# Convolution and two attentions on one core: the transformed image stored with its pixel column outside, and a new order of calls

## What is computed

```python
# block 0, image by image
perceived = conv3x3_depthwise(x, w_perc) + b_perc          # 3 filters a channel: 384 maps
hid = gelu(w_up1 @ perceived + b_up1)                      # 256
x_new = x + w_up2 @ hid + b_up2                            # 128
q, k, v = w_qkv @ x_new + b_qkv
w = softmax(q . k over the 3x3 neighbours / sqrt(128))     # zero-padded borders
h = x_new + sum(w * v)
# block 1
xn = group_norm(h, 8 groups) * gamma + beta
q, k, v = xn @ Wq + bq, xn @ Wk + bk, xn @ Wv + bv
out = softmax(q k^T / sqrt(128)) v @ Wp + bp               # 1024 x 1024 an image
y = xn + out
```

## Time and profile before

| | |
|---|---|
| three runs | 1112.1, 1113.34, 1116.12 us, median 1113.34 |
| the profiled execution | 1112.2 us, span 1110.4 us |
| mean granted clock of PE | 0.996 of 2.4 GHz |
| busy share PE, DVE, ACT, POOL | 96%, 81%, 70%, 39% |
| matmuls | 7488, of which 1728 are the convolution's, 1536 the values' |
| one turn of the loop | 65.97 us |

### The profile page before, as it was taken

One profiled execution on the slowest core, in us unless ns is written; L12 is line 12 of the kernel. 1 busy time (PEld: TensorE's weight loads), 2 busy tenths in 40 slices (PEclk: granted clock), 3 DMA queues, 4 the chain that ended last, 5 costly groups with the idle time before them and its releaser, 6 DMA issues.

```text
span 1110.4 us, 22840 instructions
## 1 busy us (share of the span) xinstructions
PE 1067.4 (96%) x7488; PEld 979.2 (88%) x7488; DVE 901.5 (81%) x1907; ACT 779.4 (70%) x1515; POOL 438.5 (39%) x399
## 2 busy tenths in 40 slices
PE   6979999999999999999999999999999999999897
PEld 5968989899898999989899898989989899998786
DVE  7868788888888878888887878888888887887875
ACT  4476767767676777767777676776767677776664
POOL 4656152542715345261532615254271534523021
PEclk9999999999999999999999999999999999999999
DMA  6001010100201010010100101010010100000000
GB/s 106 1 1 20 1 30 10 29 10 0 38 0 28 9 28 10 0 38 0 28 9 5 32 0 28 9 28 9 0 38 0 28 9 9 11 1 20 1 11 29
DMA packets 85746, 18.60 MB, mean 17 GB/s; under 512 B 67536, under 2 KB 85712, under 8 KB 85712
## 3 DMA queue, kind: packets, MB, share of 16 engines
q1 hardware_dynamic: 84992, 17.77, 8.3%
q10 hardware_dynamic: 720, 0.39, 0.2%
HBM read 9.76 MB, written 8.39 MB: 16 GB/s over the span
## 4 chain that ended last, share of the span: by engine, by line
issue 44%; PE 28%; POOL 20%; DVE 4%; ACT 3%; POOLq 1%; DMA 0%; DVEq 0%; ACTq 0%
PE work L457 7%; PE work L459 6%; PE work L458 6%; POOL g_lo L1295 6%; POOL t_lo L1295 3%; PE ps_t L614 3%; POOL v_hl L1295 2%; POOL h_lo L1295 2%; POOL xn_lo L1295 2%; PE ps_s L457 2%; PE ps_s L459 2%; PE ps_s L458 1%; POOL r_tok L1357 1%; POOL r_tok L1354 1%; POOL t_f L1312 1%
## 5 line engine op out<-in xcount | busy, mean ns | idle before, releaser
L1295 POOL TENSOR_TENSOR g_lo<-u,g_hi 128x512 fp32r<-128x512 f32 x60 | 77.8, 1303 | 375.1 <-ACT g_hi L890 375.1
L1749 DVE TENSOR_REDUCE nm<-ps_s 128x1 f32<-128x1024 f32 x124 | 151.4, 1221 | 32.5 <-PE ps_s L459 32.2
L457 PE MATMUL work<-t_lo,wc_hi 128*128 128x256 f32 x576 | 171.0, 297 | 5.1 <-POOL t_lo L1295 3.5
L991 ACT ACTIVATE et_hi<-ps_t 128x1024 fp32r<-128x1024 f32 x128 | 130.7, 1021 | 58.9 <-PE ps_t L614 57.7
L1755 DVE TENSOR_TENSOR et_lo<-ps_t,et_hi 128x1024 fp32r<-128x1024 f32 x128 | 156.0, 1219 | 17.8 <-ACT et_hi L991 14.5
L459 PE MATMUL work<-t_hi,wc_hi 128*128 128x256 f32 x576 | 165.7, 288 | 0.0
L458 PE MATMUL work<-t_hi,wc_lo 128*128 128x256 f32 x576 | 165.6, 287 | 0.0
L457 PE MATMUL work<-et_lo,vv_hi 128*128 128x256 f32 x512 | 147.3, 288 | 0.0
L459 PE MATMUL work<-et_hi,vv_hi 128*128 128x256 f32 x512 | 145.1, 283 | 0.0
L458 PE MATMUL work<-et_hi,vv_lo 128*128 128x256 f32 x512 | 144.9, 283 | 0.0
L981 ACT ACTIVATE e<-ps_s,nm 128x1024 f32<-128x1024 f32 x124 | 137.5, 1109 | 5.7 <-DVE nm L1749 5.2
(11 more groups left out here) (227 smaller groups left out, 2937.0 us busy)
## 6 DMA issues: line engine op xcount, KB each, us to landing
x_in<-in_x SPq DMA_DIRECT2D x64, 128.0 KB, 3.6
out<-r_tok SPq DMA_DIRECT2D x32, 256.0 KB, 2.3
e<-in_L_conv_w_up SPq DMA_DIRECT2D x1, 384.0 KB, 4.2
y<-in_L_conv_w_qkv SPq DMA_DIRECT2D x1, 192.0 KB, 4.8
const<-in_const ACTq DMA_DIRECT2D x1, 166.0 KB, 5.6
y<-in_L_conv_w_up ACTq DMA_DIRECT2D x1, 128.0 KB, 5.3
const<-in_const ACTq DMA_DIRECT2D x1, 64.0 KB, 3.2
bv_row<-in_L_conv_b_qkv SPq DMA_DIRECT2D x1, 64.0 KB, 2.9
```

What stands on the lines that cost most here:

```text
L457: te.matmul(dst, wh, xl, start=first, stop=False)
L991: act.activation(et_hi[:, :, (t % 4) * 128:(t % 4 + 1) * 128], ps_t[:, :].rearrange("p (k c) -> p k c", k=TILES), ACT.Copy) \
L1295: return pool.tensor_tensor(dst, full, hi, ALU.subtract)
L1749: dve.tensor_reduce(nm1[:, t:t + 1], score_tile(n, t)[:, :], AX.X, ALU.max, negate=True) \
```

## The change

**The transformed image's layout.** `t_f`, `t_hi` and `t_lo` were `[128, 6, 8, 34]` (transformed row, group of rows, column) and are `[128, 6, 34, 8]`, with the column outside and the group of rows inside. The matmul of a filter column `dx` then reads 32 columns by 8 groups as one piece of 256 elements, from `8 * dx` on. What it leaves in the bank is ordered the same way, so `take` and `product` read the bank with the column outside. The writers of `t_f` (DVE and POOL) use the old order of elements through a view and write eight elements apart; `t_hi_part` and `t_lo_part` go over the memory in its own order. Sizes, types and the number of operations stay.

**The ends.** The turn of image 0 is now part of `fill_program` and that of image 13 of `drain_program`, on each engine, each with its own order and banks. The loop runs over 2 to 12, with turn 1 before it.

**The order of calls and the banks** are new in fill, turn and drain, on all engines.

**Waits.** `local_mask_max(n, 0)` also waits for qq and kk of the image before, the first `scores` for `w1v_ready` and `biases_ready`, the first `q_hi_half` for `scaled`.

```diff
-    ("as", 0, 3), ("as", 1, 2), ("conv", 0, 1), ("conv", 1, 0), ("as", 2, 3), ("at", 0, 2), ("conv", 2, 0),
...
+    ("as", 0, 3), ("conv", 0, 1), ("as", 1, 2), ("conv", 1, 3), ("at", 0, 2), ("conv", 2, 0), ("as", 2, 1),
...
-        t_hi = sb("t_hi", [128, NT, QUADS, WP], F32R)
+        t_hi_mem = sb("t_hi", [128, NT, WP, QUADS], F32R)
         t_at = region("t_mem", NT * QUADS * WP)
-        t_f = placed("t_f", [128, NT, QUADS, WP], t_at)
-        t_lo = placed("t_lo", [128, NT, QUADS, WP], t_at, F32R)
+        t_f_mem = placed("t_f", [128, NT, WP, QUADS], t_at)
+        t_lo_mem = placed("t_lo", [128, NT, WP, QUADS], t_at, F32R)
+        t_hi, t_f, t_lo = (t.rearrange("p k w q -> p k q w") for t in (t_hi_mem, t_f_mem, t_lo_mem))
...
             fill_program()
-            turn_program(0)
-            with eng.Fori(1, B - 3) as it:
+            turn_program(1)
+            with eng.Fori(2, B - 3) as it:
                 turn_program(it)
-            turn_program(B - 3)
             drain_program()
...
                 for m in range(2):
-                    dst = bank("conv", k, n)[:, m * 256:(m + 1) * 256].rearrange("p (r w) -> p r w", r=QUADS)
+                    dst = bank("conv", k, n)[:, m * 256:(m + 1) * 256]
                     for dx in range(3):
-                        xs = [t[:, k, :, dx:dx + W] for t in (t_hi, t_lo)]
+                        xs = [t[:, k, dx:dx + W, :].rearrange("p w q -> p (w q)") for t in (t_hi_mem, t_lo_mem)]
...
-                act.activation(t_hi[:, two, :, 1:1 + W], t_f[:, two, :, 1:1 + W], ACT.Copy).then_inc(t_hi_ready.handle, 1)
+                act.activation(t_hi_mem[:, two, 1:1 + W, :], t_f_mem[:, two, 1:1 + W, :], ACT.Copy).then_inc(t_hi_ready.handle, 1)
...
                 act.activation(u_of(n)[:, :, :, row, :], bank("conv", k, n)[:, :]
-                               .rearrange("p (m r w) -> p m r w", m=2, r=QUADS), ACT.Copy).then_inc(taken.handle, 1)
+                               .rearrange("p (m w r) -> p m r w", m=2, r=QUADS), ACT.Copy).then_inc(taken.handle, 1)
...
-                return bank("conv", k, n)[:, :].rearrange("p (m r w) -> p m r w", m=2, r=QUADS)
+                return bank("conv", k, n)[:, :].rearrange("p (m w r) -> p m r w", m=2, r=QUADS)
...
+                if j == 0:
+                    for user in ("qq", "kk"):
+                        dve.wait_ge(*pe[user].after(n - 1, 1))
```

More of the change, by code:

```diff
@@ L104 @@
 DRAIN_BANK_OF = {(u, x, n): bank for u, x, n, bank in DRAIN_PLAN}
-USES = FILL_PLAN + [(u, x, it + 3 - STAGE_OF[u], bank) for it in range(B - 2) for u, x, bank in BANK_PLAN
+USES = FILL_PLAN + [(u, x, it + 3 - STAGE_OF[u], bank) for it in range(1, B - 3) for u, x, bank in BANK_PLAN
                     if it + 3 - STAGE_OF[u] < B] + DRAIN_PLAN
@@ L595, in scores @@
                 te.wait_ge(*qq_lo_ready.after(n, t // 4))
+                if is_first(n) and t == 0:
+                    te.wait_ge(*w1v_ready.after(0, 0))
+                    te.wait_ge(*biases_ready.after(0, 0))
                 te.wait_ge(*kk_lo_ready.after(n, 1))
@@ L729, in fill_program @@
                 vv(0, 1)
+                probs_t(0, 0)
+                scores(0, 1)
+                local_scores(1, 2)
+                conv(2, 0)
+                local_probs_t(1, 0)
+                scores(0, 2)
+                conv(2, 1)
+                probs_t(0, 1)
+                conv(2, 2)
+                scores(0, 3)
+                local_probs_t(1, 1)
+                local_scores(1, 3)
+                probs_t(0, 2)
+                conv(2, 3)
+                values(0, 0)
+                scores(0, 4)
@@ new lines, in fill_program @@
+                probs_t(0, 3)
+                conv(2, 4)
+                conv(2, 5)
+                local_probs_t(1, 2)
+                scores(0, 5)
+                local_values(1, 0)
+                probs_t(0, 4)
+                local_probs_t(1, 3)
+                values(0, 1)
+                local_values(1, 1)
+                up2(2, 0)
+                probs_t(0, 5)
+                group_moments(1)
+                attended(0, 0)
+                scores(0, 6)
+                final_t(0, 0)
@@ new lines, in fill_program @@
+                values(0, 2)
+                scores(0, 7)
+                probs_t(0, 6)
+                k(2, 0)
+                q(2, 0)
+                up2(2, 1)
+                probs_t(0, 7)
+                v(2, 0)
+                kk(1, 0)
+                qq(1, 0)
+                kk(1, 1)
+                values(0, 3)
+                vv(1, 0)
+                qq(1, 1)
+                scores(1, 0)
+                attended(0, 1)
+                q(2, 1)
+                v(2, 1)
+                k(2, 1)
@@ L789, in drain_program @@
             def drain_program():
+                probs_t(B - 3, 0)
+                scores(B - 3, 1)
+                local_scores(B - 2, 0)
+                conv(B - 1, 0)
+                local_scores(B - 2, 1)
+                scores(B - 3, 2)
+                probs_t(B - 3, 1)
+                conv(B - 1, 1)
+                local_scores(B - 2, 2)
+                probs_t(B - 3, 2)
+                conv(B - 1, 2)
+                local_probs_t(B - 2, 0)
+                scores(B - 3, 3)
+                local_probs_t(B - 2, 1)
@@ new lines, in drain_program @@
+                conv(B - 1, 3)
+                local_scores(B - 2, 3)
+                probs_t(B - 3, 3)
+                scores(B - 3, 4)
+                conv(B - 1, 4)
+                local_probs_t(B - 2, 2)
+                conv(B - 1, 5)
+                local_values(B - 2, 0)
+                scores(B - 3, 5)
+                local_probs_t(B - 2, 3)
+                probs_t(B - 3, 4)
+                values(B - 3, 0)
+                up2(B - 1, 0)
+                local_values(B - 2, 1)
@@ new lines, in drain_program @@
+                values(B - 3, 1)
+                group_moments(B - 2)
+                scores(B - 3, 6)
+                probs_t(B - 3, 5)
+                v(B - 1, 0)
+                k(B - 1, 0)
+                q(B - 1, 0)
+                attended(B - 3, 0)
+                scores(B - 3, 7)
+                probs_t(B - 3, 6)
+                final_t(B - 3, 0)
+                values(B - 3, 2)
+                up2(B - 1, 1)
+                qq(B - 2, 0)
+                kk(B - 2, 0)
+                kk(B - 2, 1)
@@ L1316, in t_lo_part @@
                 pool.wait_ge(*t_hi_ready.after(n, k))
-                minus(t_lo[:, two, :, 1:1 + W], t_f[:, two, :, 1:1 + W], t_hi[:, two, :, 1:1 + W].bitcast(F32)) \
+                minus(t_lo_mem[:, two, 1:1 + W, :], t_f_mem[:, two, 1:1 + W, :], t_hi_mem[:, two, 1:1 + W, :].bitcast(F32)) \
                     .then_inc(t_lo_ready.handle, 1)
@@ new lines, in fill_program @@
+                et_lo_tile(0, 3)
+                y_half(1, 0)
+                halo_lo(1, 1)
+                row_max(0, 5)
+                pt_lo_pair(1, 2)
+                pt_lo_pair(1, 3)
+                et_lo_tile(0, 4)
+                y_half(1, 1)
+                channel_moments(1)
+                a_lo_part(0, 1)
+                h_half(2, 0)
+                group_variance(1)
+                et_lo_tile(0, 5)
+                row_max(0, 6)
+                group_norm(1)
+                output(0, 0)
@@ new lines, in fill_program @@
+                row_max(0, 7)
+                a_lo_part(0, 2)
+                et_lo_tile(0, 6)
+                h_half(2, 1)
+                k_lo_half(2, 0)
+                q_lo_half(2, 0)
+                v_half(2, 0)
+                et_lo_tile(0, 7)
+                x_turn(3, 0)
+                x_turn(3, 1)
+                qq_lo_half(1, 0)
+                kk_lo_half(1, 0)
+                kk_lo_half(1, 1)
+                transform_even(3)
+                a_lo_part(0, 3)
+                qq_lo_half(1, 1)
@@ L1872, in turn_program @@
+                transform_two(3)
+                row_max(1, 0)
+                q_lo_half(2, 1)
+                v_half(2, 1)
+                transform_ends(3)
+                vv_lo_half(1, 0)
+                k_lo_half(2, 1)
+                output(0, 1)
+                vv_lo_half(1, 1)
             def turn_program(it):
```

680 lines of the change are left out of this document (478 added, 202 removed), and 50 rows, old and new, of tables (BANK_PLAN, DRAIN_PLAN, FILL_PLAN).

## The result

The changed kernel takes 1103.28 us (median of 4 runs, 1099.92 to 1104.62) beside 1114.17 for the kernel before in the same comparison: a ratio of 0.9898, 95% interval 0.9869 to 0.9927. The forecast was 1097.6, in a range of 1087 to 1109. Six more executions beside the last experiments gave a median of 1101.18 us (1100.63 to 1109.47) and a ratio of 0.9868 (0.9838 to 0.9897). So it is faster by about 1%, and it is some 6 us slower than forecast. The profiled execution took 1104.62 us, its span is 1102.2.

A forecast was written before the change was run, and what follows sets the result against it. The prediction took PE's own work in the middle as the bound. From 1112.2 us its terms gave - 8.5 - 8.0 + 2.8 + 0 - 2 = 1096.5, with 1.1 for the median 1097.6 us; range 1087 to 1109.

The forecast's parts named there:

- What bounds it now: Whole kernel: the middle is PE's own work, shortened only by fewer or quicker matmuls or less waiting.
- 1. The moving operand: Convolution on PE: one piece of 256 elements saves 5.3 ns a matmul at most, 9.2 us; 8.5 taken.
- rival B: Convolution no quicker, since breaks between rows of 32 cost nothing: 1106 us, chance 0.15.
- 2. xn_lo on POOL: Full turns: earlier xn_lo frees the second kk, h_lo for q comes late next; 8.0 us gained, between 5 and 9.2.
- Rival F: The new orders bring waits of their own and the kk wait only moves to q: 1103 us, chance 0.09.
- 3. Strided access: DVE and POOL: strided bank reads and t_f writes add 2.5 and 0.5 us a turn, mostly hidden; 2.8 us charged.
- 4. The fill: Start of the kernel: earlier fold 0 and weight transposes against later convolutions; net 0, between 4 lost and 5 gained.
- 5. The drain: End of the kernel: image 15's local scores start under image 14's; 2 us off, between 0 and 5.
- C: Strided DVE operations near the upper end make row_max and et_lo late, PE loses 0.9 us a turn: 1107, chance 0.12.
- D: POOL's transform: the pair of t_f takes 3.6 us, PE stands 0.9 us a turn: 1122 us, chance 0.08.
- Rival E: The fill gains too as the clock stays up, 5 more there and 3 from the drain: 1089 us, chance 0.10.

The follow-up runs named there:

- e1: The kernel before with only the new layout of t_hi, t_f, t_lo and the bank: 1106.97 us, ratio 0.9936.
- e3: The changed kernel with the layout of before, so only its orders, banks and two turns written out are new: 1114.45 us, ratio 0.9991.
- e4: The kernel before with one exchange on POOL, xn_lo of the second half ahead of v_lo of the first: 1112.45 us, ratio 0.9995.
- e7: The kernel before with xn_lo ahead of v_lo on POOL and score tile 7 one step earlier on PE, DVE and ACT: 1111.85 us, ratio 0.9978.
- e6: The changed kernel with 119 extra transposes that keep PE busy in its fill: 1096.78 us, ratio 0.9835.
- e9: The changed kernel with the old fill and first full turn, plus 92 extra transposes, those for ps_t in its upper half: 1090.22 us, ratio 0.9755.
- e8: The changed kernel with old fill and first full turn, 92 extra transposes, and the old last full turn and drain: 1102.05 us, ratio 0.9878.
- e10: The changed kernel itself, run again without any change: 1101.18 us (1100.63 to 1109.47, 6 runs).
- e2: The changed kernel with the fill and first full turn of the kernel before on all engines: 1095.97 us, ratio 0.9832.

## Why the prediction was right or wrong

The direction was right and the time lies in the range; it is 5.7 us above the forecast. One step failed, others gave more than was taken, and the two cancelled in part.

**What bounds it now** held: the middle is PE's own work, and turns 1 to 12 gained by less idle time and quicker steps alone.

**1. The moving operand.** Right in mechanism, the size off: -8.5 was taken; 124.9 to 118.6 ns is 6.3 x 1728 = 10.9 us, beyond the end of 9.2 that the values matmuls gave. e1 against before (65.20 against 65.94 us a turn) and the changed kernel against e3 (64.57 against 65.27) show it twice: rows of 32 elements that lie 34 apart cost 6 ns a matmul here. Why they do was not taken apart. Where a row begins is not it: in the full turns of before the steps of the three filter columns, whose rows begin one element apart, have the same median, 124 to 125 ns. L552, which rival B called as a witness, was none: its sixteen rows are one row of 32 read sixteen times. By the Trainium skill's page "SBUF — State Buffer", section "Door 1: The DMA port swizzle", as the prediction read it, rival B's time would have come out; the runs decide against that reading.

**2. xn_lo on POOL.** The size was right, -8.0: the middle turns lost 7.3 us of idle time. The reason was wrong. The step said that the exchange on POOL frees kk and that h_lo for q is next. e4 shows that the exchange alone frees nothing: e of tile 7 was as late and stood hidden behind xn_lo; e7 shows a third wait, for the bank of qq. The new orders of PE, ACT, DVE and POOL together remove them; which of the moved calls are needed for that was not taken apart. h_lo was late in no full turn. Rival F's mechanism, a wait that only moves, is what happened in the old orders; in the new ones it did not.

**3. Strided access.** +2.8 was charged; in a full turn it costs nothing on PE (0.05 us idle), the low end. DVE went from 54.64 to 56.55 us a turn, 1.9 more, where 2.5 was taken, but most of that is not the layout: over turns 1 to 12 e1 has DVE busy for 0.45 us a turn more than before, and e3, which has the orders without the layout, for 1.4 (the last section has the largest part of that). Reads of the bank eight elements apart are free (684 and 679 ns), the writes of t_f are not. By the page "Vector Engine (DVE) Microarchitecture Reference" of the Trainium skill, section "Measured stream behaviour on trn2", the estimate was 0.75 us more per u operation; the trace has 0.00. That section measures operands in SBUF, and what a u operation reads eight elements apart lies in a PSUM bank. For t_f's writes, which go to SBUF, the trace has 0.26 and 0.19 us more over 256 columns, 0.7 to 1.0 ns a column. In the fill, where the transform is on the path, e1 has two new waits of 0.4 us.

**4. The fill.** This is the step that failed. It said net 0, between 4 lost and 5 gained. With the parts of steps 1 and 2 that lie in it, turn 1 should have started some 2 us earlier than before; it started 9.3 later. Two things were missed. The order: I put conv(0,5) 1 to 2 us later and had missed conv(0,4). DVE ends fold_rest(5) at 36.8 where it ended it at 31.2, wc_lo(4) (the lower half of the folded weights of transformed row 4) stands behind it and starts at 36.7 instead of 33.8, and PE waits 2.78 us for it. conv(0,5) starts at 41.88 instead of 38.40. The order costs 5.7 us in all by e6 and e9, of which 3.0 are there when conv(1,0) starts; which of the moved calls behind it carry the rest was not taken apart. The clock: I charged it 3.4 us as a fixed cost of the chain "that the new order keeps". It is not fixed. It fell behind each of the three idle stretches of 2 us or more and again from 78 on, and what runs at the lower clock comes later for it (5.2 us by e6, which took the idle stretches away). I had one profiled execution of before, in which it fell once, and took that for the rule.

**5. The drain.** The new order gives 3.3 by e8, and 3.2 by e10 against e1 at the same clock (150.61 and 154.44, less the 0.6 of the one wait), so -2 was near. In the first profiled execution of the changed kernel the clock at the end took it back: from turn 13 on it gained 1.1 us, which is no more than one turn's 1.37 of layout and wait.

The rivals: B, C and D did not occur (118.6 ns, PE idle 0.05 us a turn, t_f on POOL 0.75 to 1.0 us). Rival E's fill did not occur in the changed kernel either, though e9 shows that it was to be had: with the clock up it took 1090.22, beside E's 1089. The forecast's own errors cancelled in part. For turns 1 to 12 its parts add up to 10.8 us of gain (6.4 of the convolution, 6.8 of the wait, less 2.4), and 16.35 was measured: some 5 us too little. For the fill with turn 0 they make 2 of gain, and 9.3 was lost: 11 us too little loss. That the time lies no further off than 5.7 us is in part luck.

## What to carry to other kernels

Where PE waits once a turn, look for what would be late right behind that wait before counting it as gain: undo it alone on the chip, and price an order inside the orders that it comes with. In this fill an idle stretch of PE cost twice, once as a wait and once as lower clock in what followed: a few matmuls into a bank that is free anyway, shorter than the wait that they fill, gave the changed kernel 4 to 7 us and made its executions agree within 1 us. And take the fill of one kernel and the middle of another where their programs hold the same calls up to a turn's boundary: the old fill under the new rest was 5 to 7 us better than the whole that had been chosen (e2), and 11 to 13 us better with PE kept busy in it as well (e9).

## What the runs showed of the hardware

The clock after idling. The kernel before took 1111.6 to 1114.4 us with mean clocks of 0.995 to 0.996 and 1117.4 to 1120.7 with 0.984 to 0.987, the same program each time. In the profiled executions it falls to 0.5 behind stretches in which PE did little, as behind 64 to 66 us above. It does not always fall there: in the profile of before PE waits 2.79 us up to 21.65 and 2.15 up to 62.19, and the clock stays at 1.00 until 78; in that of e1 the same 2.8 us were followed by 0.57 from 22 to 26. With PE kept busy (e6, e9) it did not fall in the fill at all.

A small operation beside POOL. halo_lo, 32 partitions x 128 elements, takes 289 ns alone and 1.29 us when POOL's first addition of the residual (r_tok<-vv_hi,vv_lo) starts just ahead of it, which the new orders bring about once a turn (timelines of DVE and of POOL):

```profile
398.93 1.29 DVE L1963 TENSOR_TENSOR pt_lo<-halo_t,pt_hi 32x128 fp32r<-32x128 f32 x1
...
398.72 1.35 POOL L1612 TENSOR_TENSOR r_tok<-vv_hi,vv_lo 128x512 f32<-128x512 f32 x1
```

Its group went from 9.2 to 21.3 us of busy time, 12 of DVE's additional 28, and it cost PE nothing in the full turns (0.05 us idle). It looks as if the one had waited for the other to end; the Trainium skill's page "SBUF — State Buffer", section "SBUF: two separate sides", has an exclusive lock on a pair of ports for such a pair of operations. The trace agrees with that; no run here took it apart.
